# The fourth quarter sum of a seven-product block on GpSimd instead of VectorE (four graph layers, 8192 nodes, Trainium2)

## The reference

```
h = relu(layernorm(x)); for k in 0, 1: h = tanh(concat(adj @ h, h) @ W0[k]);  x += h
h = relu(layernorm(x)); x += adj @ (h @ W1) + bias
h = relu(layernorm(x)); x += adj @ (h * (u >= 0.1) / 0.9)
h = relu(layernorm(x)); x += concat(h, (adj @ h) / (sum(adj, 1) + 1)) @ W3.T
```

## Time and profile before

| | us |
|---|---|
| median of 3 runs | 2234.13 |
| profiled execution, its own time | 2234.12 |
| its span, first to last instruction | 2232.3 |
| TensorE (PE) busy | 2201.4 |
| VectorE (DVE) busy | 1649.0 |
| ScalarE (ACT) busy | 171.6 |
| GpSimd (POOL) busy | 9.8 |
| GB/s of all transfers, mean | 376 |

### The profile page before, as it was taken

One profiled execution on the slowest core, in us unless ns is written; L12 is line 12 of the kernel. 1 busy time (PEld: TensorE's weight loads), 2 busy tenths in 40 slices (PEclk: granted clock), 3 DMA queues, 4 the chain that ended last, 5 costly groups with the idle time before them and its releaser, 6 DMA issues.

```text
span 2232.3 us, 36846 instructions
## 1 busy us (share of the span) xinstructions
PE 2201.4 (99%) x15326; PEld 1177.2 (53%) x15326; DVE 1649.0 (74%) x3238; ACT 171.6 (8%) x384; POOL 9.8 (0%) x22
## 2 busy tenths in 40 slices
PE   6999999999999999999999999999999999999999
PEld 3555555555554346666654566666344444444446
DVE  7477777777888877877752678787765877787776
ACT  1000000000003321111100000000110100000000
POOL 0000000000000000000000000000000000000000
PEclk9999999999999999999999999999999999999999
DMA  9999999999999789999999998889999999999997
GB/s 397 421 420 416 421 421 412 411 401 406 395 376 366 295 314 331 340 339 340 341 380 333 334 341 317 350 336 367 361 394 409 377 421 420 398 385 421 413 398 306
DMA packets 118613, 838.35 MB, mean 376 GB/s; under 512 B 14000, under 2 KB 16304, under 8 KB 17072
## 3 DMA queue, kind: packets, MB, share of 16 engines
q1 hardware_dynamic: 114336, 831.57, 94.0%
q10 hardware_dynamic: 3344, 2.33, 0.3%
q0 software_dynamic: 768, 2.10, 0.3%
HBM read 833.85 MB, written 2.10 MB: 374 GB/s over the span
## 4 chain that ended last, share of the span: by engine, by line
PE 93%; DVE 4%; DMA 2%; issue 1%; ACT 0%; DVEq 0%; ACTq 0%
PE double_acc L916 39%; PE single_acc L888 17%; PE single_acc L944 15%; PE spare L916 14%; PE spare L888 6%; DMA store<-in_adj 2%; PE natural L1008 1%; DVE store L1354 0%; DVE store L1355 0%; DVE stack L1273 0%; DVE stats L1151 0%; DMA resid<-in_x 0%; DVE partial L1254 0%; DVE deg_part L1202 0%; DVE deg_quarter L1206 0%
## 5 line engine op out<-in xcount | busy, mean ns | idle before, releaser
L916 PE MATMUL double_acc<-store,operand 128*64 128x512 f32 x4336 | 964.8, 593 | 1.3 <-ACT operand L1119 1.3
L916 PEld LDWEIGHTS double_acc<-store,operand 128*64 128x64 f32 x4336 | 335.3, 137 | 518.6 <-issue 496.0
L888 PE MATMUL single_acc<-store,operand 128*64 128x256 f32 x3696 | 439.3, 382 | 20.6 <-DVE operand L1187 12.4
L888 PEld LDWEIGHTS single_acc<-store,operand 128*64 128x64 f32 x3696 | 293.6, 138 | 189.4 <-issue 89.5
L944 PE MATMUL single_acc<-store 128*64 128x256 f32 x1888 | 364.3, 380 | 0.0
L944 PE MATMUL single_acc<-store,operand 128*64 128x256 f32 x1416 | 329.3, 380 | 3.4 <-DVE store L1356 3.3
L916 PE MATMUL spare<-store,operand 128*64 128x512 f32 x1456 | 330.3, 592 | 0.6 <-DMA store<-in_adj 0.6
L1254 DVE TENSOR_TENSOR partial<-spare,partial 64x256 f32<-64x256 f32 (+1 forms) x248 | 125.5, 506 | 180.7 <-PE spare L916 112.3
L944 PEld LDWEIGHTS single_acc<-store 128*64 128x64 f32 x1888 | 229.2, 137 | 34.9 <-issue 2.1
L944 PEld LDWEIGHTS single_acc<-store,operand 128*64 128x64 f32 x1416 | 188.9, 137 | 67.5 <-issue 33.9
L916 PEld LDWEIGHTS spare<-store,operand 128*64 128x64 f32 x1456 | 125.1, 137 | 149.8 <-issue 142.0
(11 more groups left out here) (79 smaller groups left out, 895.7 us busy)
## 6 DMA issues: line engine op xcount, KB each, us to landing
store<-in_adj SPq DMA_DIRECT2D x791, 1024.0 KB, 8.3
for_layer<-in_u POOLq DMA_DIRECT2D x16, 128.0 KB, 5.5
out_rows<-resid ACTq DMA_DIRECT2D x15, 128.0 KB, 5.8
resid<-in_x SPq DMA_DIRECT2D x2, 512.0 KB, 6.0
resid<-in_x SPq DMA_DIRECT2D x1, 1024.0 KB, 13.8
out_rows<-resid ACTq DMA_DIRECT2D x2, 64.0 KB, 1.7
w_stack<-in_w_both ACTq DMA_DIRECT2D x2, 32.0 KB, 8.8
ident<-in_identity ACTq DMA_DIRECT2D x1, 64.0 KB, 16.4
```

The costliest lines, as they stand in the source:

```text
L888: last = nc.tensor.matmul(acc[half_of(h), 0:HALF], operand[:, b.j * TPB + t, half_of(b.row.half)], stream[:, t, nodes_of(h)], start=b.firs ...
L916: last = nc.tensor.matmul(acc[half_of(half), :], operand[:, b.j * TPB + t, half_of(half)], stream[:, t, :], start=b.first and t == 0, stop ...
```

## The change

`t4` is no longer made by VectorE but by GpSimd. VectorE's L1355 (L1363 in the new file) does not end in `link` any more but raises a new semaphore `second_sum_made`. GpSimd walks `PLAN` too: at each "sums7" it waits for the block's load and for that semaphore, makes `t4` and raises `sums_made`. Its 16 loads of `u` stand in the same walk, each behind the step "post" of the row two before its own; they keep their wait for `norm_ready`.

```
         operand_combined = sem("operand_combined")
         sums_made = sem("sums_made")
+        second_sum_made = sem("second_sum_made")
...
             pool.memset(w_stack[:, 2:4, :], 0.0).then_inc(weights_cleared, 1)
             pool.memset(deg_quarter[:, :], 0.0).then_inc(deg_cleared, 1)
-            for row in ROWS:
-                if row.sweep == 3:
+            for what, of in PLAN:
+                if what == "sums7":
+                    n, at = SEVEN_BLOCKS.index(of), LOAD_OF[of.number].slot * SLOT
+                    _, t2, t4 = block_sums(of)
+                    wait_loaded(pool.wait_ge, of)
+                    pool.wait_ge(second_sum_made, n + 1)
+                    nc.gpsimd.tensor_tensor(t4, inside(at + 2 * BLOCK, (BLOCK, 2)), t2, ALU.subtract).then_inc(sums_made, 1)
+                elif what == "post" and 2 * NB <= of.r + 2 < 3 * NB:
+                    row = ROWS[of.r + 2]
                     pool.wait_ge(norm_ready, row.r - 1 - NB)
                     pool.dma_start(u_in[:, row.r % 2], u[:, tiles(row.i), :]).then_inc(u_loaded[row.r % 2], 16)
...
-                y21, y22 = inside(at + 2 * BLOCK, (BLOCK, 2)), inside(at + 2 * BLOCK + HALF, (BLOCK, 2))
-                t1, t2, t4 = block_sums(b)
+                y22 = inside(at + 2 * BLOCK + HALF, (BLOCK, 2))
+                t1, t2, _ = block_sums(b)
                 link(nc.vector.tensor_tensor(t1_t3, y12_y22, y11_y12, ALU.subtract))
-                link(nc.vector.tensor_tensor(t2, y22, t1, ALU.subtract))
-                nc.vector.tensor_tensor(t4, y21, t2, ALU.subtract).then_inc(sums_made, 1)
+                nc.vector.tensor_tensor(t2, y22, t1, ALU.subtract).then_inc(second_sum_made, 1)
```

## The result

The changed kernel takes 2266.05 us, the median of 4 runs (2265.97 to 2267.83), the kernel before on the same chip 2234.15. The ratio is 1.0145, with a 95% interval from 1.013 to 1.016. The forecast was 2265.5, between 2243 and 2275.

What follows compares the result with a forecast made beforehand. TensorE bounds the kernel, with a two-buffer sums loop without slack. Loop 17.1, heads 12.0, one slack row 0.4 and loop under turns 1.9 gave +31.4 us on 2234.12: 2265.5, range for 8 in 10 2243 to 2275.

Steps and rivals of the forecast that it cites:

- TensorE and the loop: Late in a row, the two-buffer loop has no slack (6.11 against TensorE's 6.04); additions are paid once per two blocks.
- Sizes in the loop: Late in a row: hand-over 0.12, subtraction 1.17, loop 6.67 instead of 6.11; 30 x 0.57 = +17.1 us.
- The rows of even length: Eight rows ending on a block whose L1354 waits some 0.25 for GpSimd's subtraction: 8 x 0.24 = +1.9 us.
- the upper bound of 1.39: GpSimd's subtraction with two inputs and one output, each its own pass: 0.10 + 3 x 0.43 = 1.39 us.
- the 1.12: GpSimd's subtraction as a quarter of the Trainium skill's 4497 ns for 2048 elements; the loop term would be 15.6.
- Turns: At SBUF, VectorE's two-input instructions and GpSimd's subtraction alternate, instruction by instruction; chance 0.48, predicted time 2265.5 us.
- side by side: Rival: VectorE and GpSimd read SBUF at once, so row-head waits shrink by 2.7; 2248.5 us, chance 0.38.
- Size at the heads: At nine row heads the third block's sums come 1.33 us later: +12.0 us.
- The row with 0.96 of slack: One more row head, with 1.80 idle where the nine have 0.84: pays 0.4 us.
- The 3.4 us given as the most that could come back in this stretch: Stretch of all seven-product rows: TensorE busy 746.6 of 750 us, so no more than 3.4 us can come back.
- The loads of `u`: GpSimd's 16 issues of 0.54 ahead of the third block's subtraction: cost 0; uncovered 8.6 us.

Runs made afterwards that it cites:

- e1: Changed kernel, but GpSimd makes `t4` only from a row's fifth seven-product block on (54 blocks), VectorE for the first four: 2256.18 us, ratio 1.0098.
- e8: Kernel before (VectorE makes `t4`) with a third buffer for `t1`, the wait for the block two before moved behind L1354: 2232.23 us, ratio 0.9991.
- e4: Changed kernel plus one wait: VectorE starts a row's fourth block's sums only when GpSimd has finished the third's: 2259.58 us, ratio 1.0114.
- e5: Kernel before, with GpSimd doing an idle scratch subtraction for each seven-product block that nobody waits for: 2272.67 us, ratio 1.0173.
- e9: Changed kernel (GpSimd makes every `t4`) with a third buffer for `t1`: 2253.75 us, ratio 1.0089.
- e6: Kernel before, with GpSimd doing two idle clears of 600 elements for each seven-product block, which read nothing in SBUF: 2234.42 us, ratio 1.0001.
- e10: GpSimd makes `t4` for a row's first two seven-product blocks only, plus a third buffer for `t1`: 2229.98 us, against 2234.30 before, ratio 0.9981.
- e7: Kernel before with only GpSimd's 16 loads of `u` walked in the common order: 2234.18 us, ratio 1.0000.
- e3: Changed kernel, but GpSimd makes `t4` only for a row's first two seven-product blocks (32 blocks): 2231.81 us, ratio 0.9989.
- e2: Changed kernel, but GpSimd makes `t4` only for a row's first four seven-product blocks (64 blocks): 2246.69 us, ratio 1.0056.

## Why the prediction was right, step by step

**TensorE and the loop: right.** What the change added to the chain from one block's end to the sums of the block two later was paid in full, once for two blocks. e1 isolates it, e8 shows that the loop was already limiting before, and the number of waits is 30 as counted. They last 0.5 and 0.3 and not 0.6 each; the rest of a round's 0.68 doesn't show as idle time.

**Sizes in the loop: somewhat low.** Hand-over 0.15 for 0.12, subtraction 1.27 for 1.17: the loop is 6.79 instead of 6.67. With 30 places of 0.68 the term is 20.4 for 17.1. The rows of even length add 8 x 0.2 = 1.6 for 1.9. The subtraction's 1.27 lies about halfway between the 1.17 that I took and the upper bound of 1.39 (both inputs and the output, a pass each); the 1.12 that I gave beside it was too low as well.

**Turns: right, and the mechanism shown.** The lean of 0.48 against 0.38 was a choice; e4, e5 and e9 leave no room for side by side. On GpSimd's side a subtraction is concerned and a clear is not (e5, e6).

**Size at the heads: high.** Nine heads lose 1.02 and not 1.33: 9.2 for 12.0. VectorE comes to the third block 0.50 earlier (13.05 from the first block's sums, 993.82 less 980.77, where it was 13.55) and not 0.25. GpSimd holds L1363 for 0.95 (1.64 less 0.69), not for all of its 1.27.

**Two small terms were wrong.** The row with 0.96 of slack paid nothing (0.04) where I had 0.4. The first row of sweep 2 paid 0.68 where I had nothing. The sums of its first block ended 1.09 before TensorE's first product (806.49 and 807.58), and that was not enough: behind the next L1362 the subtraction ends only at 808.05, and the product starts at 808.19. I had not looked up that row. The 3.4 us given as the most that could come back in this stretch was wrong too, though nothing in the sum rests on it (e10).

**The loads of `u`: right**, 0 (e7).

The sum, 17.1 + 12.0 + 0.4 + 1.9 = 31.4, came within 0.5 us of the 31.9 measured because the loop was 3.3 low and the heads 2.8 high. The mechanisms earned a time near this one; that it came within 0.5 us was luck.

## What to carry to other kernels

An engine with spare time isn't a free engine: look at the chain that the moved instruction stands in. Here two buffers made a loop without slack, so 0.68 us more latency was paid in full 30 times, while 0.71 us of VectorE time saved per block was worth nothing there. GpSimd and VectorE took turns at SBUF where GpSimd's subtraction met a VectorE instruction with two inputs there (2.11 us for 1.27, and 1.64 for 0.69). So give GpSimd what isn't urgent and falls beside one-input work (e3), and look at what VectorE has queued right behind the signal.

## What the runs showed of the hardware that I had not expected

TensorE's clock. In the kernel e2, 2.30 us of waiting (1434.05 to 1436.35) is followed by a stretch at a granted clock of 0.59, a mix of the levels of 2.4 and 1.2 GHz:

```profile
1436.00:1440.00 4.00, 3.65 (x20) 2.62 (x22) 0.75 (x1) 0.00 (x0) 1.47 (x2) 0.59 1.03 432
```

The same happens one row earlier, after 2.31 us up to 1391.92. In the changed kernel waits of the same length at the heads of the same two rows, up to 1405.81 and 1450.12, are followed by full clock. The first of them:

```profile
1405.00:1410.00 5.00, 4.19 (x40) 3.41 (x42) 2.12 (x2) 0.00 (x0) 1.93 (x2) 1.00 1.02 429
```

Each fall costs about 1.7 us: e2's runs lie at 2245.8 and 2247.5, 1.7 and 3.4 above the 2244.1 that its waits explain, and one run of the changed kernel lies 1.8 above the others. In the profile of e9 both waits of this length brought a fall, and in e5 one of two waits of 2.97. No wait of 1.8 us or less behind the start was followed by one in these profiles. Why one such wait brings it and another doesn't stays open; no run was made on it.
